# Position values ahead of the turn, and the gate's products around the queries, in the mixing steps of a decoder layer

## The reference

```
pos_values = x @ Wpv + bpv
pos_ret    = (cos * cumsum(cos * pos_values) + sin * cumsum(sin * pos_values)) / sqrtD
key_ph     = tanh(x @ Wk + bk) * pi
kv_values  = x @ Wkv + bkv
gh         = gelu(concat([x, shift1(x)]) @ Wg1 + bg1)      # the gate's hidden layer
gates      = sigmoid(gh @ Wg2 + bg2)
kv_ret     = (cos(key_ph) * cumsum(...) + sin(key_ph) * cumsum(...)) / ...
bw         = softmax(gelu(x @ Wb1 + bb1) @ Wb2 + bb2)
blended    = bw[0] * pos_ret + bw[1] * kv_ret
x1         = layernorm(2 * x + layernorm(blended) @ Wo + bo)
q          = x1 @ xWq + xbq                                # queries of the cross attention
```

## Time and profile before

| | |
|---|---|
| median of 3 runs | 2133.51 us (2129.97 to 2135.98) |
| the profiled execution | 2140.03 us, its span 2138.3 us |
| granted TensorE clock, mean over the span | 0.963 |
| TensorE busy / weight loads | 1976.8 us (92%) / 1054.4 us |
| VectorE, ScalarE, GpSimd busy | 1703.2, 1498.3, 761.1 us |

### The profile page before, as it was taken

How to read it: one execution, slowest core, us unless ns; L and a number is a source line. 1 busy time by engine, 2 the same in 40 slices (tenths; PEclk the granted TensorE clock), 3 DMA queues, 4 the chain that set the end, 5 groups by cost and what they waited for, 6 DMA issues and landing times.

```text
span 2138.3 us, 43534 instructions
## 1 busy us (share of the span) xinstructions
PE 1976.8 (92%) x11070; PEld 1054.4 (49%) x11070; DVE 1703.2 (80%) x3237; ACT 1498.3 (70%) x4232; POOL 761.1 (36%) x1103
## 2 busy tenths in 40 slices
PE   7989899899999999999999999899639999999994
PEld 3545455423322233322322332333439999999993
DVE  5889976699999999999999999999435555554554
ACT  4655565799999999999999999999303233233333
POOL 0112112244444444444444442142443333333332
PEclk9989989999999999999999999999859999999997
DMA  4112103957677676766768576754642222222224
GB/s 160 45 45 74 59 25 100 210 127 106 127 121 128 136 102 131 130 119 121 112 136 139 111 132 137 142 96 94 188 101 37 37 35 37 37 37 35 37 37 170
DMA packets 135743, 211.13 MB, mean 99 GB/s; under 512 B 41146, under 2 KB 104378, under 8 KB 134474
## 3 DMA queue, kind: packets, MB, share of 16 engines
q1 hardware_dynamic: 107864, 150.18, 38.8%
q0 software_dynamic: 26240, 59.00, 10.5%
q10 hardware_dynamic: 1554, 1.05, 0.2%
HBM read 136.40 MB, written 73.74 MB: 98 GB/s over the span
## 4 chain that ended last, share of the span: by engine, by line
PE 41%; ACT 28%; issue 14%; DVE 10%; DMA 3%; POOL 1%; SPq 1%; ACTq 1%; DVEq 0%; POOLq 0%
ACT w_all L1940 24%; PE psum L2191 12%; PE psum L2201 11%; PE psum L674 7%; DVE neg_max L1760 6%; PE psum L1571 2%; PE psum L1512 2%; POOL list_all L341 1%; DMA area<-x_all 1%; PE psum L2178 1%; PE psum L899 1%; PE psum L701 1%; DMA kst<-k_parts 1%; ACT w_all L1029 1%; DMA v_all<-w_all 1%
## 5 line engine op out<-in xcount | busy, mean ns | idle before, releaser
L1940 ACT ACTIVATE w_all<-psum,neg_max 128x512 f32<-128x512 f32 x1600 | 1077.3, 834 | 22.3 <-DVE neg_max L1760 19.8
L1760 DVE TENSOR_REDUCE neg_max<-psum 128x1 f32<-128x512 f32 x1600 | 978.9, 678 | 8.7 <-PE psum L1571 8.2
L1940 ACT ACTIVATION_READ_ACCUMULATOR w_all<-psum,neg_max 128x1 f32 x1600 | 565.5, 353 | 0.0
L1571 PE MATMUL psum<-qst,kst 96*128 96x512 bf16 x1536 | 469.1, 384 | 34.2 <-ACT w_all L1940 27.6
L2240 ACT ACTIVATE hid<-psum,b 128x128 f32<-128x128 f32 x568 | 162.3, 369 | 386.2 <-PE psum L2191 386.2
L1512 PE MATMUL psum<-w_all 128*32 128x512 f32 x3072 | 410.8, 607 | 3.9 <-POOL w_all L1834 2.5
L1571 PEld LDWEIGHTS psum<-qst,kst 96*128 96x128 bf16 x1536 | 121.0, 97 | 533.7 <-ACT w_all L1940 489.7
L1834 POOL TENSOR_TENSOR w_all<-vst,inv 128x64 f32<-128x64 f32 x384 | 109.3, 291 | 536.4 <-DVE inv L1674 531.6
L2191 PE MATMUL psum<-xst,w 128*128 128x128 f32 x2272 | 267.6, 276 | 0.0
L2191 PEld LDWEIGHTS psum<-xst,w 128*128 128x128 f32 x2272 | 261.8, 193 | 0.1
L2201 PE MATMUL psum<-area,hid 128*128 128x256 f32 x1136 | 256.9, 379 | 0.0
(11 more groups left out here) (238 smaller groups left out, 2041.0 us busy)
## 6 DMA issues: line engine op xcount, KB each, us to landing
kst<-k_parts SPq DMA_DIRECT2D x384, 112.0 KB, 6.6
k_parts<-w_all POOLq DMA_DIRECT2D x52, 336.0 KB, 4.0
w_all<-in_W SPq DMA_DIRECT2D x16, 1024.0 KB, 10.4
area<-in_ctxT SPq DMA_DIRECT2D x16, 896.0 KB, 4.7
qst<-q_parts SPq DMA_DIRECT2D x192, 64.0 KB, 6.0
v_all<-area POOLq DMA_DIRECT2D x13, 896.0 KB, 4.7
vst<-v_all SPq DMA_DIRECT2D x31, 224.0 KB
q_parts<-spare POOLq DMA_DIRECT2D x24, 256.0 KB, 3.0
```

Source lines behind the costliest of these rows:

```text
L1571: last = pe.matmul(psum[:, 2 * sbuf + i, :], kst[:, h, j, t * P:(t + 1) * P], qst[:, h, j, :], start=True, stop=True)
L1760: v.tensor_reduce(neg_max[:, sbuf, i:i + 1], psum[:, 2 * sbuf + i], AX_X, ALU.min) \
L1940: act.activation(odd_probs if odd else probs_at[pb][:, j, :], psum[:, 2 * sbuf + i, :], ACT.Exp, bias=neg_max[:, sbuf, i:i + 1], scale=-1. ...
```

## The change

In a step with `front`, the first piece of the position values (`project(5, wpv, ..., range(1))`) is issued ahead of `turn(e)`, with its wait for `pv_used`. The first piece of the gate's hidden layer (bank 2) is issued between the turn and the queries. The second (bank 3) is cut into its first two chunks, between the queries and `less(e, 0)`, and its last two, behind `less(e, 0)`. The program of no other engine is changed, and the numbers of matmuls are the same.

```diff
+                def project_part(bank, weights, rhs, ks, chunks):
+                    for k in ks:
+                        last = pe.matmul(psum[:, bank, :], weights[:, k, P:2 * P], rhs(k), start=k == 0,
+                                         stop=k == chunks - 1)
+                    return last
...
                     if drain:
                         for j in range(VJ):
                             unit_v(0, j)
+                    if front:
+
+                        pe.wait_ge(pv_used, c + 1)
+                        project(5, wpv, now(1 - h), C, range(1))
                     if end:
                         turn(e)
                     if front:
 
-                        pe.wait_ge(pv_used, c + 1)
-                        project(5, wpv, now(1 - h), C, range(1))
+                        pe.wait_ge(kv_used, c + 1)
+                        project(2, wg1, now(1 - h), 2 * C, range(1))
                     if drain:
                         for j in range(2):
                             unit_v(1, j)
                     if end:
                         queries(e)
                     if front:
-
-                        pe.wait_ge(kv_used, c + 1)
-                        project(2, wg1, now(1 - h), 2 * C, range(1))
+                        project_part(3, wg1, now(1 - h), range(C), 2 * C)
...
                     if end:
                         less(e, 0)
                     if front:
-                        project(2, wg1, now(1 - h), 2 * C, range(1, C)).then_inc(gh_ready, 1)
+                        project_part(3, wg1, now(1 - h), range(C, 2 * C), 2 * C).then_inc(gh_ready, 1)
```

## The result

The changed kernel takes 2116.67 us (median of 5 runs, 2113.39 to 2120.52) against 2133.51 us (2129.97 to 2135.98): the ratio is 0.9913, 95% interval 0.9896 to 0.9931, or 16.8 us less. The forecast was 2124.3 us in a range from 2119.0 to 2129.5: the right side, and about half of the gain.

What follows compares the result with a forecast made beforehand. The bound was a 41.24 us loop, changed in the half TensorE and ScalarE share. 6 x 1.16 = 6.96, less 0.80 for late turns, plus 3.06 clock: 9.2 off 2133.5 gives 2124.3 us, range 2119 to 2129.5.

Steps and rivals of the forecast that it cites:

- The path: From turn to keys on TensorE and ScalarE: 14.88 us against 16.04, a gain of 1.16 us a step, 6.96 in six.
- the wait ahead of the second `less`: TensorE waits about 0.6 us for ScalarE's second split; said to cost nothing, since the keys wait for the third split anyway.
- that rival: ScalarE's table load between first and second split costs its 1.28 us row once more: 1.5 us slower, 2135.0; chance 2%.
- The copy of x1: Needed by the queries after the turn; covered by 8 instructions it costs nothing, without that cover under 1 us.
- VectorE did not take over: Rival: VectorE's margin before `mix_out` falls from 2.1 to 1.0; losing 2 us a step removes the gain, 2133.5; chance 5%.
- The late turns: Wpv's 1.72 us exceeds the idle ahead of three turns by 0.28, 0.24 and 0.28: 0.80 us lost together.
- the clock's term: TensorE's low clock after two turns: 1.70 and half of 2.73 come back, 3.06 us, bounds 0 and 4.43.
- steps 7 and 8: Steps 0, 7 and 8 keep their order; what follows step 6 hangs on the chain and moves along.
- The rival of the late turn: Low clock lasts until the turn, Wpv takes 3.44, turn 2.0 us late: 5.0 us slower in six, 2138.5; chance 5%.
- that of the chain's gain alone: Rival: low clock comes as often after the turns as before; gain 6.2 us, 2127.3; chance 16%.
- the clock's bound of one trace: All the low-clock loss after two turns comes back, 4.43 us, making the whole gain 11.4 us.
- an allowance of 2 us: Error allowed in the median, added at both ends of the range, 2129.5 and 2119.

Runs made afterwards that it cites:

- the filler: Kernel before, with the first piece of the position values also made once ahead of the turn in steps 1 to 6: 2127.85 us, ratio 0.9966.
- the two finer cuts: Changed kernel with the gate's second piece whole before the first `less`: 2124.46 us; changed kernel with the gate's first piece halved around the queries: 2114.67 us.
- the repeat: The changed kernel run again unaltered for a second trace, on another chip's before of 2135.12 us: 2120.61 us, ratio 0.9930.

## Why the prediction was wrong

**The path held.** 1.16 us a step were forecast, and 23.20 - 21.92 = 1.28 measured; the steps in between (the wait ahead of the second `less` 0.64 against 0.6, 1.29 to the gelu, keys 14.76 after the turn) are all in the trace. The table load costs its own row and no more, 1.29 us from its start to the gelu, so that rival falls. The copy of x1 would have cost more than the "under 1 us" without its cover: 1.11 where only the values were moved. The forecast's path is not quite the chain's: the wait for the second split, said to cost nothing, is on it, level with the third split. VectorE did not take over: no idle stands ahead of `mix_out` (L727) in any of the six steps.

**The late turns were oversized.** 0.80 was taken off. Two turns of six had no idle left, not three, and L718 to turn is then 18.15 and 18.18 us instead of 18.03: 0.27 in all. TensorE begins the next matmul before the recorded end of the one before, so an idle of 1.44 in the rows holds nearly the whole of 1.72.

**The step that failed is the clock's term:** "So I take the first back in full (1.70) and half of the second (1.36): 3.06". The mechanism was right and the size was not. In the trace that the prediction read, all of it comes back, 4.4 us; in the other two traces of before the hits cost 5.5 and 8.0, so their mean is 6.0, twice the term. 0 of 12 turns are hit in the two traces of the changed kernel, with gaps up to 3.08 us, and 0 of 18 in those of the filler and the two finer cuts, against 7 of 18 in the three of before. Beside this, the sentence that steps 7 and 8 "get no other order" left out that the clock can change the time of a step with the same order: the seventh turn was 1.2 us late in two traces of three before, and in neither after. Whether the new order did that is not shown, since the turn was late in the filler's trace too, with no turn hit.

By the first pair of traces the sum at the seventh turn is 6 x 1.28 = 7.7, less 0.3, plus 4.4 from the hit turns, plus 1.2 = 13.0; measured 328.96 - 315.99 = 13.0. Over all traces the seventh turn comes at a mean of 330.7 before (three) and 316.2 after (two, 315.99 and 316.47), 14.5 us apart, and the spans' means are 2135.1 and 2118.6, 16.5 apart. So nearly nine tenths of the gain are there at the seventh turn, and at the eighth, 369.5 against 354.2, it is 15.2. What comes behind it changes from run to run: the chain's wait for the landing of `v_all` is 11.45, 7.58 and 9.77 us in the three traces of before, 8.44 and 10.78 in the two after, and these five show no tie to the order; the landing itself comes 15.2 earlier by the means. The first pair of traces is 23.4 us apart in span, 10 of them behind the seventh turn, and overstates the change. Whether the last 1 or 2 us of the medians' 14.5 to 16.8 have a cause behind the mixing stage stays open.

The gains of the single edits do not add up to that of both: filling the gap alone 7.3, values ahead alone 7.6, gate alone -8.1, both 14.5 to 16.8. Each piece needs the other. Putting the values ahead is worth 7.6 by itself and 22.6 with the gate's new order (2143.19 - 2120.61): 6 x (23.63 - 21.92) = 10.3 of that is path, and some 12 are the five turns that are no longer hit, 1.71 in one and 2.67 to 2.76 in the four others.

The rival of the late turn fell; so did that of the chain's gain alone, which would have been 6.2. The range failed since its lower end added the clock's bound of one trace to an allowance of 2 us (2133.5 - 11.4 - 2 is 2120.1; the 2119 stated lies 1.1 below its own terms), where the three traces of before hold clock losses of 5.6, 5.5 and 9.2 us up to the seventh turn (hits and late seventh turn together: 1.69 + 2.69 + 1.2; 2.80 + 2.68; 2.71 + 2.57 + 2.72 + 1.2). By the repeat's 14.5 us the result would have stood at the very end of the range, so how far it was missed is partly the luck of the runs; that the gain was sized too small is not, since both pairs of medians and the traces say so. The sum of the chances holds one slip: the case of the late turn, 5.0 us slower, was counted as slower although it lies within the 6.4 us of no change.

## What to carry to other kernels

A wait of TensorE of a few microseconds costs nothing by the chain of waits and can still cost the microseconds behind it: look at what the same instructions take behind each wait, and price a move into the gap by both. A clock loss that hits some steps and not others must not be priced from one trace; the filler, a matmul product made twice, shows in one experiment whether the medians hold such a loss. Where two engines pass work back and forth, cut independent work into pieces just shorter than the other engine's part, and put each where that engine is busy.

## What the runs showed of the hardware

The length of the gap ahead of a turn told in most cases whether the clock fell behind it. Over all traces of the kernels here, gaps of 4.45 to 4.79 us ahead of the six turns were followed by the 1.2 GHz level each time (ten of ten: one, two and three in the traces of before, four in the gate's alone), those of 3.09 and 3.10 as well (two of two), and those of 3.07 and 3.08 not (none of two). Of the shorter gaps only those were followed by it that had 1.11 us more of idle behind the turn, and not all of these: one of 2.74 where only the values were moved (the other five there were 1.38 and were not), and two of 2.00 at the seventh turn, in the second trace of before and in the gate's alone, where the queries took 5.20 and 5.30 instead of 3.70.

The gaps are themselves made by the clock. In the step ahead of 160.11 it fell during the second product of the statistics (L735), and the gap was 1.44; in the step ahead of 242.61 it held, and the gap was 4.79. TensorE's timeline of before, and windows of it (columns as in the earlier trace rows, the granted clock third from the end):

```profile
148.13 2.70 PE L735 MATMUL psum<-mean_w,w_all 128*128 128x1 f32 x16
150.69 6.26 PE L674 MATMUL psum<-w_all 128*128 128x512 f32 x8
...
230.64 1.93 PE L735 MATMUL psum<-mean_w,w_all 128*128 128x1 f32 x16
232.42 3.68 PE L674 MATMUL psum<-w_all 128*128 128x512 f32 x8
...
148.00:150.00 2.00, 2.00 (x16) 2.00 (x16) 0.00 (x0) 1.98 (x3) 0.00 (x0) 0.77 0.00 0
150.00:152.00 2.00, 2.00 (x6) 1.48 (x7) 0.67 (x3) 1.96 (x5) 0.00 (x0) 0.50 0.00 0
...
230.00:232.00 2.00, 2.00 (x20) 2.00 (x20) 0.00 (x0) 2.00 (x3) 0.00 (x0) 1.00 0.00 0
```

The gaps of 2.76 and 3.10 stand between the two: there L735 still took 1.93, and the values' products behind it 5.38. So a clock held high in one half of a step was paid for in the other half, until matmuls stood in the gap. The filler shows that this is why a step with more work was faster. The first window also shows that the clock fell while TensorE's rows read fully busy (2.00 of 2.00), in a row of products of one column; what in that row let it fall no run here shows.
